# Experts on routed tokens only: slot tiles sorted by expert, rows scattered and results gathered through memory, in the period of the same image

## The reference

```python
x = x + mixer(ln(x), W)              # relu(cos similarity) ** 2, over all tokens of an image
t = ln(x); p = softmax(t @ gate_w + gate_b)
top_p, top_i = top_k(p, 2); top_p = top_p / sum(top_p)
dispatch = sum(one_hot(top_i) * top_p)                 # token x 16, two entries not zero
hidden = silu(t @ w1[e]) * (t @ w2[e])                 # for each expert e, 64 -> 128
x = x + sum over e of dispatch[:, e] * (hidden @ w3[e])
x = x + deformable_conv(ln(x))       # offsets by a 3 x 3 convolution, 4 corners a tap, mask
x = x + routed_ffn(ln(x))            # 64 -> 256 -> 64, gelu, top half by x @ wr
```

## Time and profile before

| | us |
|---|---|
| median of three timed runs | 4189.94 |
| the three runs | 4177.14, 4191.68, 4189.94 |
| span of the profiled execution (its own time is not listed apart from it) | 4742.8 |
| median as a share of that span | 0.8834 |
| TensorE busy | 3689.9, 78% |
| VectorE busy | 3096.6, 65% |
| ScalarE busy | 2394.1, 50% |
| GpSimd busy | 1954.9, 41% |

### The profile page before, as it was taken

One profiled execution on the slowest core, in us unless ns is written; L12 is line 12 of the kernel. 1 busy time (PEld: TensorE's weight loads), 2 busy tenths in 40 slices (PEclk: granted clock), 3 DMA queues, 4 the chain that ended last, 5 costly groups with the idle time before them and its releaser, 6 DMA issues.

```text
span 4742.8 us, 58643 instructions
## 1 busy us (share of the span) xinstructions
PE 3689.9 (78%) x21912; PEld 1953.7 (41%) x21912; DVE 3096.6 (65%) x4834; ACT 2394.1 (50%) x4144; POOL 1954.9 (41%) x1805
## 2 busy tenths in 40 slices
PE   6889868888788878889788888889788888864432
PEld 2334434444444444444444444444544444433421
DVE  5466457766677566766577567766577576664765
ACT  5656644466445654466445664456444664431210
POOL 0000344526255343535255353544345354446661
PEclk8999979999799978999799888989799988975555
DMA  3000222222122221222122221231222222233436
GB/s 99 8 1 1 73 59 60 65 66 79 51 65 68 70 72 57 67 73 71 51 65 66 70 77 55 64 86 51 55 71 72 71 71 57 60 89 89 111 97 125
DMA packets 374811, 314.93 MB, mean 66 GB/s; under 512 B 312672, under 2 KB 317024, under 8 KB 374528
## 3 DMA queue, kind: packets, MB, share of 16 engines
q0 software_dynamic: 85248, 231.33, 16.5%
q1 hardware_dynamic: 289280, 79.88, 7.9%
HBM read 279.30 MB, written 57.69 MB: 71 GB/s over the span
## 4 chain that ended last, share of the span: by engine, by line
PE 54%; DVE 14%; ACT 9%; another core or an unknown queue 9%; issue 7%; DVEq 3%; DMA 2%; POOL 2%; SPq 1%; ACTq 0%
PE PS L1487 49%; DVE work L866 3%; PE PS L1690 3%; DVEq L488 2%; ACT work L1379 2%; DVE G L492 2%; POOL G L448 2%; PE PS L1522 1%; ACT work L1308 1%; DVE G L486 1%; DVE st L454 1%; DVE small L862 1%; DVE work L777 1%; DMA out<-x 1%
## 5 line engine op out<-in xcount | busy, mean ns | idle before, releaser
L448 POOL DMA_INDIRECT G<-corner_table,index x1800 | 1954.3, 1086 | 2651.6 <-DVE value L494 1256.1
L1379 ACT ACTIVATE work<-PS,descale 128x512 f32<-128x512 f32 (+2 forms) x896 | 565.5, 633 | 638.0 <-PE PS L1487 510.6
L866 DVE SCALAR_TENSOR_TENSOR work<-PS,descale,work 128x512 f32<-128x512 f32 (+2 forms) x896 | 604.8, 681 | 385.0 <-ACT work L1379 276.1
L1308 ACT ACTIVATE work<-PS 128x768 f32<-128x768 f32 (+2 forms) x800 | 650.5, 823 | 374.3 <-PE PS L1487 251.0
L777 DVE TENSOR_TENSOR work<-work 128x768 f32<-128x768 f32 (+2 forms) x496 | 481.1, 973 | 440.2 <-PE PS L1487 280.3
L1487 PE MATMUL PS<-xn_hl,xn_hh 128*128 128x384 f16 (+2 forms) x1600 | 550.8, 345 | 121.8 <-ACT work L1308 76.3
L1487 PE MATMUL PS<-work,xm 128*64 128x400 f32 (+3 forms) x3200 | 642.1, 514 | 0.4 <-DVE work L777 0.4
L486 DVE TENSOR_TENSOR G<-G,corner_w 128x768 f32<-128x768 f32 x600 | 559.8, 951 | 55.9 <-DMA G<-corner_table,index 53.4
L1487 PE MATMUL PS<-xn_hl,xn_ll 128*128 128x384 f16 (+2 forms) x1600 | 546.7, 342 | 0.0
L1487 PE MATMUL PS<-work,w3s 128*64 128x384 f32 (+2 forms) x1792 | 466.8, 600 | 85.6 <-DVE small L862 80.8
L1487 PE MATMUL PS<-xn_hl,w1h 128*128 128x512 f16 (+2 forms) x896 | 331.1, 370 | 157.5 <-DVE work L866 131.3
(11 more groups left out here) (258 smaller groups left out, 4959.1 us busy)
## 6 DMA issues: line engine op xcount, KB each, us to landing
G<-corner_table,index POOLq DMA_INDIRECT x1800
corner_table<-rows_scratch SPq DMA_DIRECT2D x32, 784.0 KB
corner_table<-G SPq DMA_DIRECT2D x8, 841.0 KB, 8.5
xin<-x SPq DMA_DIRECT2D x8, 768.0 KB, 5.3
rows_scratch<-xln SPq DMA_DIRECT2D x8, 768.0 KB
x_scratch<-xB SPq DMA_DIRECT2D x8, 768.0 KB
yw_scratch<-yw SPq DMA_DIRECT2D x7, 784.0 KB
x<-x_scratch SPq DMA_DIRECT2D x4, 784.0 KB
```

Of the source, the lines that this page charges most:

```text
L448: GP.indirect_dma_start(G[0:rows, n % 2, tap * 4 * C:(tap + 1) * 4 * C], None, tables[b % 2], bass.IndirectOffsetOnAxis(ap=index[0:rows, c ...
L866: V.scalar_tensor_tensor(hid[:, e % 4, 0:w], S[2 + e % 2][:, 0:w], descale[:, MOE2:MOE2 + 1], silu[:, e % 2, 0:w], ALU.mult, ALU.mult).the ...
L1308: A.activation(relu[0:rows, u % 2, :, 0:n], PS[u % 2][0:rows, :, 0:n], ACT.Relu).then_inc(s["relu_done"], 1)
L1379: A.activation(silu[:, e % 2, 0:w], S[e % 2][:, 0:w], ACT.Silu, scale=descale[:, MOE1:MOE1 + 1]).then_inc(s["silu_done"], 1)
```

## The change

The experts get tokens sorted by expert. A slot tile is 128 rows of one expert; 64 of them (`SLOT_TILES` = 2T + E - 2) hold every assignment of an image, two a token. `gate` now keeps the two hot places of each token (`hot`). `positions` counts on TensorE, by 26 matmuls with a triangular matrix and with ones, how many tokens of the same expert stand ahead. `route` (VectorE) makes of it the slot of each assignment (`slot`) and the expert of each slot tile (`expert_of`). GpSimd scatters the normalised rows (f16 high and low parts, `split_a`) into `slot_rows` in memory, 50 indirect DMAs; SP loads them back in four pieces (`load_slots`). The experts then run over 16 groups of four slot tiles: `turn_over` transposes four tiles, `up` loads the four expert numbers into registers of TensorE's queue and multiplies by the weights at those addresses, `down` multiplies by `w3s` and leaves rows of tokens. ScalarE copies the result to `slot_y`, SP stores it (`store_slots`), and GpSimd gathers for each token its two rows (`gather_results`, 50 indirect DMAs). VectorE's `combine` multiplies by the two shares and adds.

The program is cut into nine units. A unit u has a mixer (an idle one for u = 8) and 19 turns (8 in the last). In the mixer of u stand `combine` and `geo_start` of image u-1 (bodies 4 and 5), its geometry (bodies 7 on), the weighing of tiles 17 to 22 and the samples of tiles 16 to 21 of image u-2. Each turn weighs one tile and samples one: tiles 23 and 24 of image u-2 in turns 0 and 1, then tiles 0 to 16 of image u-1. Normalisation and gate of image u stand in turns 0 to 4, its routing in turn 5, the FFN of image u-3 in turns 3 to 6, the expert steps two a turn in turns 10 to 18, the stacks of image u+1 in turn 18. The image is kept in four buffers (`xq`) instead of two.

The similarities come from two operands instead of three (`xn_hl` and `xn_lh`, 14 chunks of stacks). VectorE makes 62 of 100 relus, straight from the banks, ScalarE the other 38 and all squares. All tiles are sampled in one form, without a transpose back.

The core of the diff:

```diff
+            def load_slots(i):
+                sp.wait_ge(s["scattered"], 2 * T * 16 * (i + 1))
+                if i >= 1:
+                    sp.wait_ge(s["combined"], i)
+                    sp.wait_ge(s["om_taken"], 2 * i)
+                if i >= 3:
+                    sp.wait_ge(s["fdown_done"], 4 * (i - 2))
+                for q in range(PIECES):
+                    sp.dma_start(slot_x[:, q * PIECE:(q + 1) * PIECE, :], slot_piece(slots_dram, q)).then_inc(slots_in[q], 16)
...
+            def store_slots(i):
+                for q in range(PIECES):
+                    sp.wait_ge(s["y_taken"], GROUPS // 2 * i + GROUPS // 2 // PIECES * (q + 1))
+                    sp.dma_start(slot_piece(y_dram, q), slot_y[:, q * PIECE:(q + 1) * PIECE, :]).then_inc(s["y_stored"], 16)
...
+                if u + 1 < B:
+                    sp.wait_ge(s["x1_added"], 4 * (u + 1))
+                    load_x(u + 1)
+                if valid(u):
+                    load_slots(u)
+                if valid(u - 3):
+                    store_yw(u - 3)
+                if valid(u):
+                    store_slots(u)
...
+            def scatter_rows(i, n):
+                t, j = n // 2, n % 2
+                rows = tile_rows(t)
+                GP.indirect_dma_start(slots_dram, bass.IndirectOffsetOnAxis(ap=slot[0:rows, i % 2, j * T + t:j * T + t + 1], axis=0),
+                                      split_a[0:rows, t, :], None).then_inc(s["scattered"], 16)
+
+            def scatter_first(i, n):
+                if n == 0:
+                    pool.wait_ge(s["slots_ready"], i + 1)
+                scatter_rows(i, n)
...
+            def gather_results(i):
+                pool.wait_ge(s["y_stored"], PIECES * 16 * (i + 1))
...
+            def unit(u):
+                if valid(u - 1):
+                    gather_results(u - 1)
+                if valid(u - 2):
+                    for t in range(LATE, T):
+                        gather_tile(u - 2, t)
+                if not valid(u - 1):
+                    for n in range(2 * T):
+                        scatter_first(u, n)
+                if valid(u - 1):
+                    for t in range(LATE if u - 1 < LAST else T):
+                        gather_tile(u - 1, t)
+                        if valid(u):
+                            for n in scatters_after(t):
+                                scatter_first(u, n)
...
+                if step == 0:
+                    dve.wait_ge(s["y_gathered"], 2 * T * 16 * (i + 1))
+                    for p, t in whole_and_last():
+                        for j in range(2):
+                            V.tensor_tensor(token_y[p, j, t, :], token_y[p, j, t, :], bc(g[p, j, t], 2, C), ALU.mult)
+                dve.drain()
+                if step == 1:
+                    for p, t in whole_and_last():
+                        V.tensor_tensor(token_y[p, 0, t, :], token_y[p, 0, t, :], token_y[p, 1, t, :], ALU.add)
+                if step == 2:
+                    for p, t in whole_and_last():
+                        ins = V.tensor_tensor(x[p, t, :], x[p, t, :], token_y[p, 0, t, :], ALU.add)
+                    ins.then_inc(s["combined"], 1)
...
+            def beside_mixer(k, j, u):
+
+                for step in range(3):
+                    if valid(k - 1) and (j, u) == (4, 3 * step):
+                        combine(k - 1, step)
+                    if valid(k - 1) and (j, u) == (5, 3 * step):
+                        geo_start(k - 1, step)
+                if valid(k - 1):
+                    geo_prepare(k - 1, j - 7, u)
+                if valid(k - 3):
...
-                                dve.wait_ge(s["relu_done"], g + u + 1)
...
-                                V.tensor_tensor(sq[0:rows, u % 4, :, 0:n], relu[0:rows, u % 2, :, 0:n], relu[0:rows, u % 2, :, 0:n],
-                                                ALU.mult).then_inc(s["sq_dve"], 1)
...
+                                dve.wait_ge(s["sim_done"], g + u + 1)
+                                if g + u > 1:
+                                    dve.wait_ge(s["squared"], g + u - 1)
+                                V.tensor_scalar(relu[0:rows, u % 2, :, 0:n], PS[u % 2][0:rows, :, 0:n], 0.0, None,
+                                                ALU.max).then_inc(s["relu_dve"], 1)
...
+            def route(k):
...
+                tt(c, D1[0:TP, 0:T * E].rearrange("p (t e) -> p t e", e=E), bc(base, 1, T), ALU.add)
+                for j, o in enumerate((o1, o2)):
+                    tt(p, o, c, ALU.mult)
+                    rd(smallc[:, j, :], p, ALU.add)
+                V.tensor_copy(slot[:, k % 2, 0:T], smallc[:, 0, :])
+                V.tensor_copy(slot[:, k % 2, T:2 * T], smallc[:, 1, :]).then_inc(s["slots_ready"], 1)
...
+            def turn_over(i, g):
+
+                if g:
+                    pe.wait_ge(s["slot_ready"], i * GROUPS + g)
+                if g % (GROUPS // PIECES) == 0:
+                    pe.wait_ge(slots_in[g // (GROUPS // PIECES)], 16 * (i + 1))
+                for n in range(4):
+                    ins = mm(Y0[:, n * TP:(n + 1) * TP], slot_x[:, 4 * g + n, :], ident16[:, :])
...
+                experts = expert_numbers(i, g)
+                for n, e in enumerate(experts):
+                    x = slot_cm[:, g % 2, n * TP:(n + 1) * TP]
+                    for h, l, o in ((w1h, w1l, S[g % 2]), (w2h, w2l, S[2 + g % 2])):
+                        mm(o[:, n * TP:(n + 1) * TP], of_expert(h, e), x, True, False)
+                        ins = mm(o[:, n * TP:(n + 1) * TP], of_expert(l, e), x, False, True)
...
+            def down(i, g, experts):
+                for n, e in enumerate(experts):
+                    at = (g % 2 * 4 + n) * C
+                    ins = mm((Y1, D1)[m % 2][:, at:at + C], hid[:, g % 4, n * TP:(n + 1) * TP], of_expert(w3s, e))
...
+            def of_expert(w, e):
+                return w[:, bass.ds(e, 1), :].rearrange("p a n -> p (a n)")
...
+                pe.wait_ge(s["hot_ready"], k + 1)
+                mm(D1[0:TP, 0:(T + 1) * E], tri_all[:, :], hot[:, :], True, False)
+                for t in range(T):
+                    later = hot[:, t * E:(t + 1) * E].unsqueeze(1).to_broadcast([TP, T - t, E])
+                    ins = mm(D1[0:TP, (t + 1) * E:(T + 1) * E].rearrange("p (t e) -> p t e", e=E), ones_all[:, :], later, False, t == T - 1)
...
+            def turn(k, r, experts):
+                b, t = turn_sample(k, r)
+                if turn_holds(k, b):
+                    for stage in range(3):
+                        sample(b, t, stage, FILL)
...
+                if k < B and r == ROUTE_TURN:
+                    positions(k)
+                if valid(k) and r == MOE_TURN:
+                    if valid(k - 3):
+                        pe.wait_ge(s["gelu_done"], (k - 2) * 2 * NCH)
+                        pe.wait_ge(s["fout_read"], 4 * (k - 2))
+                    if k < B:
+                        pe.wait_ge(s["slots_ready"], k + 1)
+                    pe.wait_ge(s["expert_ready"], k + 1)
+                for g in moe_steps(r):
+                    if valid(k):
+                        if g < GROUPS:
+                            turn_over(k, g)
+                        if 1 <= g <= GROUPS:
+                            experts[g - 1] = up(k, g - 1)
+                        if g >= 2:
+                            down(k, g - 2, experts[g - 2])
                 if k + 1 < B:
```

1103 lines of the change are left out of this document (565 added, 538 removed).

## The result

The changed kernel takes 4702.67 us (median of four runs, 4700.54 to 4705.69), the kernel before 4184.06 (four runs): a ratio of 1.1243, 95% interval 1.1225 to 1.1262. It is 12.4% slower; the prediction was 4280 us, 2% slower, with a range from 4000 to 4530.

What follows compares the result with a forecast made beforehand. TensorE was taken to set the pace between images, GpSimd with VectorE behind the last. 4742.8 profiled us with −30, −29, +22, +16 and +122 gave 4844, times 0.8834: 4280 us, range 4000 to 4530.

Steps and rivals of the forecast that it cites:

- I sum in profiled us and multiply at the end: Whole kernel: terms added in profiled us, then 4844 multiplied by 0.8834, timed median over profiled span, giving 4279.
- The mixer: Similarity stage of a late image: 224.5 less 10 for samples, plus 6 of waiting and 8 of VectorE work, 229 us.
- The wait of `combine`: VectorE in body 4 waits for the 50 result gathers, relus queued behind: 0 to 13 us, taken as 6.
- The gate: From the mixer's end M through normalisation, gate and routing to `slots_ready`: M+76, between M+66 and M+79.
- Two more weighs now stand in it (10): Added VectorE work inside the gate's stretch ahead of `slots_ready`: two weighs, 10 us.
- Scatters and tiles: GpSimd after `slots_ready`: fifty scatters (67.5 us) and three tiles between their blocks (36.6), ending at M+180.
- The expert turns: Nine turns of two expert steps, between GpSimd's tile of 12.2 and TensorE's 15.1: 13.0 us each, 117, to M+304.
- The tail's: After the last image's experts: result gathers and eight late tiles come before its first gather; tail grows by 122 profiled us.
- the sign to look for: Sign that the forecast is right: the last image's first weigh comes some 205 us behind its experts.
- Rival 1: Faster: indirect DMAs issue at 1.25 us, mixer hides its waits, −42 a period, 4040 us; chance 0.35.
- Rival 2: Slower: TensorE at 1.2 GHz, addresses and loads unhidden, its queue sets turns of 17 to 18 us, 4515 us; chance 0.17.
- The load of the expert numbers: On TensorE's queue in each expert step: one load put at 0.2 us, like a branch, beside 20 address operations at 0.035.

Runs made afterwards that it cites:

- the second profile: The kernel before, unchanged, profiled once more as the first experiment: span 4184.9 us, measured 4186.44 us, ratio 1.0006.
- the stray: The first profiled execution of the kernel before, unchanged, from which the prediction's rows were taken: span 4742.8 us.
- the earlier route: Changed kernel with logits, gate and routing a turn or two earlier, position matmuls ahead of the FFN's, scatters from tile 2, experts in turns 8 to 16: 4652.72 us.
- fixed experts: Changed kernel with a fixed expert for each slot tile, so no expert numbers loaded and no weight addresses computed on TensorE's queue: 4700.42 us, ratio 1.1235.
- a warmer TensorE: Changed kernel with 12 filler matmuls of 400 columns ahead of each sample's wait on TensorE: 4751.79 us, ratio 1.1358.

## Why the prediction was wrong

**The step that failed** is "I sum in profiled us and multiply at the end", by 0.8834. The sum itself, 4844 profiled us, stands 3% above the changed kernel's span of 4700.6, and for that kernel the ratio of time to span is 1.000. The 0.8834 was not a property of profiling, but of one execution with longer waits. The durations that most of the sum is made of, 1.25 us from gather to gather, 0.97 a square, were those of the second profile too; scaling them by the ratio of a stray made the changed kernel 12% too fast. Unscaled, the same sum gives 4844 against 4190, 15.6% slower, 3.2 points from the ratio measured. By periods, the forecast was 546 against 541.6, or +4.4 us; the runs show 532.3 against 465.0, or +67. That the unscaled sum comes so close is in part luck: it contains the stray's lengths in the mixer and the gate (30 and 10 us a period too much) and in the tail (33), and terms that were too small by 28 us a period make up for most of that. The rows gave no ground for the scaling: the change lives on a chain of GpSimd's issues, and no row said that such a chain is shorter in a timed run.

The terms, against the changed kernel's image 5, counted as in the prediction from M, the end of the mixer, where the last addition to the image ends (2683.1; 11.7 us behind the last similarity matmul):

| | predicted | measured |
|---|---|---|
| mixer | 229 | 212.5 |
| slots_ready | M+76 (66 to 79) | M+81.2 |
| last scatter | M+180 | M+189.0 |
| first experts | M+187 | M+196.8 |
| an expert turn | 13.0 | 12.5 |
| last experts | M+304 | M+309.7 |
| period (image 5 alone; the mean of five is 532.3) | 546 | 534.0 |
| tail, changed | 668 | 637.1 |

In the changed kernel's timelines these are the end of the mixer, slots_ready, the last scatter, and the first and the last matmuls of `up`:

```profile
2682.56 0.55 DVE L962 TENSOR_TENSOR xq<-xin,PS 128x384 f32<-128x384 f32 x1 [1.91 <-PE PS L1686]
...
2764.09 0.17 DVE L1048 CAST slot<-smallc 128x25 uint32<-128x25 f32 x1
...
2871.19 0.90 POOL L545 DMA_INDIRECT slot_rows<-split_a,slot  x1 [0.30 <-issue]
...
2879.89 2.21 PE L1686 MATMUL PS<-work,experts_w 128*128 128x128 f16 x16
...
2990.54 2.27 PE L1686 MATMUL PS<-work,experts_w 128*128 128x128 f16 x16 [0.17 <-issue]
```

*The mixer* was too long because its base, 224.5, was the stray's; the second profile has 194.9. What the change adds to it was too small: +4.5 in the sum, +17.6 measured. The wait of `combine` was put at 6 of a possible 0 to 13 and measured 13.0 in image 5. The experiment that halves the gathers takes 17 us out of the similarities, with what else it leaves out, and brings them to 182.6 in image 5, about the 181.4 before; so the waits for the gathers are about all that the similarities lost, net of what they saved. The edit that moves `combine` gets 6.

*The gate* was too short by 5 us, and by more in what was added: of its 76 us, 44.4 are the earlier trace rows, with the stray's wait of 13.15 us in them. The same stretch takes 34.0 in the second profile, so the change added 47 where 32 were counted. Between M and slots_ready VectorE also stands idle for gathers, ahead of weighs that are queued in front of the gate: 7.77 and 6.36 us. "Two more weighs now stand in it (10)" counted their work and not their waits. Timeline of VectorE in image 5 of the changed kernel:

```profile
2716.92 2.70 DVE L618 TENSOR_TENSOR G<-G,corner_w 128x768 f32<-128x768 f32 x3 [7.77 <-DMA G<-corner_table,index]
...
2730.21 2.70 DVE L618 TENSOR_TENSOR G<-G,corner_w 128x768 f32<-128x768 f32 x3 [6.36 <-DMA G<-corner_table,index]
...
2758.01 0.18 DVE L1027 TENSOR_SCALAR counts_i<-PS 128x16 int32<-128x16 f32 x1 [3.99 <-PE PS L1686]
```

The third row is `route`, waiting 4 us for the one-hot matmuls, which stand behind the FFN's chunks on TensorE. The experiment with the earlier route takes that and two weighs away and gets 20 us.

*Scatters and tiles* were priced right: 1.35 was taken, 1.34 is what a scatter gives back. The sum let nothing hide them, and nothing does.

*The expert turns* were bounded by the tile, as forecast: 12.5 us beside tiles, 3.9 (35.0 for nine) with nothing beside them and fixed experts.

*The tail's* growth was forecast as +122 and is +125; its level was too high by the stray's 33. The last image's first weigh comes 211 us behind the experts; the sign to look for was 205 (in the earlier trace rows it starts 84.4 behind them, which the prediction took as 86).

*The rivals.* Rival 1 (faster) asked for 1.25 us an issue and for waits hidden in the mixer; the issues came close (the 50 scatters of image 0 take 64 us, 1.28 each), the waits did not. Rival 2 named the right direction and the wrong cause: its 4515 would have been nearer, but a warmer TensorE and a queue without addresses gave nothing (4751.79 and 4700.42). TensorE's granted clock did fall: 0.50 beside the scatters, where it is busy for 20%, 0.60 in the expert turns. The Trainium skill ("TensorE: Matmul & The Clock Gate", Part 1: the throttled clock is the default and activity releases it) agrees with these rows. At 0.60 the turns took 12.5 us all the same, and not the 15.1 that the prediction worked out for 1.2 GHz, since GpSimd's tile paces them.

The load of the expert numbers, put at 0.2 us, and the address operations, put at 0.035, stand in the changed kernel's trace (ns min/median/max):

```profile
L1915 PEldq TENSOR_LOAD <-expert_of x128: 327/332/1042, 323.1 to 4060.7; - x128
...
L1686 PEldq FUSED_REGOPS  x2560: 46/46/52, 323.7 to 4065.9; - x197
```

One load and its 20 address operations are 0.332 + 20 x 0.046 = 1.25 us on the queue, and fixed experts gave back 17.1 / 16 = 1.07 us of them where TensorE bounds. The Trainium skill ("DMA: Bandwidth & Descriptors", Latency and other measured facts) has a floor of about 600 ns for such a load; the 332 ns measured here are below it, and the measurement decides.

## What to carry to other kernels

Before anything is summed from a profile, compare its span with the timed runs. If they differ, find out whether durations or waits differ, and don't scale durations by the ratio of the two. A change that takes work from the bounding engine and pays with a serial chain (route, scatter, load, compute, store, gather) is priced by that chain's length in its own period, not by the total of any engine: here the 50 scatters an image stood on its path whole, at 1.34 us each, and the result gathers for about half (25 fewer took 17 us out of the similarities and 31 out of the tail), while no engine was busy for two thirds of the time.

## What the runs showed of the hardware that was not expected

An indirect DMA costs GpSimd about the same in the three forms used here: from issue to issue in the changed kernel, in the median, a corner gather of 128 rows of 1 KB takes 1.251 us, a scatter of 128 rows of 256 bytes 1.264 and a result gather of rows of 256 bytes 1.249. The time from a scatter's issue to its landing was 2.2 us in the median. And two profiled executions of one kernel can differ by 13% with the durations of their squares, relus and gathers equal within 2.5%, and those of large groups of matmuls up to 5.5% longer in the slower one. A load of four register values from on-chip memory took 332 ns on TensorE's queue, in the median of 128.
